# Four-layer transformer on one core: the third attention unrolled, with second k and v buffers, projections spread over all heads and the rotary add moved from Pool to the vector engine

## The reference

```
q = einsum('bim,ghmd->bghid', x, w_aq)     # 4 groups x 4 heads, head size 128
k = einsum('bim,gmd->bgid', x, w_ak)       # one k and v per group
v = einsum('bim,gmd->bgid', x, w_av)
q, k = rope(q), rope(k)                    # even*cos - odd*sin, even*sin + odd*cos
s = einsum('bghid,bgjd->bghij', q*c, k*c)  # causal mask, then softmax over j
r = einsum('bghij,bgjd->bghid', softmax(s), v) @ w_ao
```

## Time and profile before

| | us |
|---|---|
| median of 3 runs | 1525.63 (1524.83 to 1525.65) |
| profiled execution, span from first to last instruction | 1523.4 |
| PE busy | 1347.9 (88%) |
| DVE busy | 740.1 (49%) |
| ACT busy | 618.9 (41%) |
| Pool busy | 113.5 (7%) |

### The profile page before, as it was taken

One profiled execution on the slowest core, in us unless ns is written; L12 is line 12 of the kernel. 1 busy time (PEld: TensorE's weight loads), 2 busy tenths in 40 slices (PEclk: granted clock), 3 DMA queues, 4 the chain that ended last, 5 costly groups with the idle time before them and its releaser, 6 DMA issues.

```text
span 1523.4 us, 21462 instructions
## 1 busy us (share of the span) xinstructions
PE 1347.9 (88%) x6802; PEld 820.4 (54%) x6802; DVE 740.1 (49%) x1677; ACT 618.9 (41%) x1516; POOL 113.5 (7%) x115
## 2 busy tenths in 40 slices
PE   5888888579999996888888889998999999999995
PEld 3633344352345454545455557765666666666863
DVE  4676545431222224776767675024433433434547
ACT  2534433479721111444344342134444444444033
POOL 2410000320000000111111110000000000000000
PEclk9989999759999999999999999999999999999998
DMA  5000000300010001000000000101000000000000
GB/s 138 1 2 1 2 18 0 143 1 0 1 66 0 0 0 73 11 11 7 14 7 14 4 8 0 58 17 61 21 21 10 21 21 10 21 21 1 1 1 28
DMA packets 17558, 31.75 MB, mean 21 GB/s; under 512 B 3049, under 2 KB 15177, under 8 KB 16356
## 3 DMA queue, kind: packets, MB, share of 16 engines
q1 hardware_dynamic: 17076, 28.94, 5.6%
q0 software_dynamic: 432, 2.16, 0.7%
HBM read 32.11 MB, written 1.05 MB: 22 GB/s over the span
## 4 chain that ended last, share of the span: by engine, by line
PE 61%; issue 23%; DVE 8%; ACT 3%; POOL 3%; SPq 0%; DMA 0%; POOLq 0%; DVEq 0%; ACTq 0%
PE bank L719 9%; PE bank L833 8%; PE bank L746 6%; PE bank L729 5%; PE bank L694 5%; PE bank L714 4%; PE bank L853 4%; PE bank L613 3%; PE bank L597 3%; PE bank L738 3%; POOL R L436 2%; PE bank L514 2%; DVE W L1315 1%; PE bank L885 1%; PE bank L568 1%
## 5 line engine op out<-in xcount | busy, mean ns | idle before, releaser
L1393 DVE TENSOR_REDUCE nm<-bank 128x1 f32<-128x128 f32 (+3 forms) x256 | 124.7, 487 | 200.0 <-PE bank L730 199.8
L909 ACT COPY R<-bank 128x512 f32<-128x512 f32 (+4 forms) x184 | 107.6, 609 | 273.9 <-PE bank L694 113.7
L719 PE MATMUL bank<-XNT,W 128*128 128x512 f32 x416 | 203.8, 614 | 16.1 <-POOL R L436 12.4
L1054 ACT ACTIVATE R<-bank,nm 128x128 f32<-128x128 f32 (+3 forms) x256 | 137.9, 539 | 173.7 <-DVE nm L1393 173.5
L729 PE MATMUL bank<-R 128*128 128x128 f32 (+3 forms) x512 | 182.5, 440 | 0.8 <-DVE R L1422 0.8
L746 PE MATMUL bank<-PT,R 128*128 128x512 f32 (+3 forms) x512 | 151.3, 438 | 2.5 <-issue 2.5
L1402 DVE TENSOR_SCALAR R<-R,erec 128x128 f32<-128x128 f32 (+3 forms) x256 | 132.7, 518 | 9.0
L738 PE MATMUL bank<-identf,R 128*128 128x128 f32 x640 | 112.8, 275 | 24.7 <-DVE R L1402 22.6
L746 PEld LDWEIGHTS bank<-PT,R 128*128 128x128 f32 x512 | 93.9, 191 | 74.9 <-issue 54.6
L1017 ACT ACTIVATE PT<-bank 128x512 f32<-128x512 f32 (+3 forms) x256 | 109.7, 519 | 47.4 <-PE bank L602 41.4
L909 ACT COPY PT<-bank 128x128 f32<-128x128 f32 (+3 forms) x256 | 110.7, 434 | 40.7 <-PE bank L738 40.3
(11 more groups left out here) (196 smaller groups left out, 1698.5 us busy)
## 6 DMA issues: line engine op xcount, KB each, us to landing
W<-in_wq SPq DMA_DIRECT2D x32, 128.0 KB, 2.0
W<-in_wo SPq DMA_DIRECT2D x2, 2048.0 KB, 8.1
W<-in_wk SPq DMA_DIRECT2D x20, 128.0 KB, 2.1
W<-in_wv SPq DMA_DIRECT2D x20, 128.0 KB, 2.0
W<-in_wa SPq DMA_DIRECT2D x2, 1024.0 KB, 5.4
W<-in_wb SPq DMA_DIRECT2D x2, 1024.0 KB, 7.2
W<-in_ed SPq DMA_DIRECT2D x1, 1792.0 KB, 14.6
W<-in_eg SPq DMA_DIRECT2D x1, 1760.0 KB, 7.0
```

Source lines behind the costliest of these rows:

```text
L719: ins = mm(bank[:, :], wqkv23[:, 0 if kind == "q" else 1, c, :], XNT[:, c, b * SEQ:(b + 1) * SEQ], start=c == 0, stop=c == DC - 1)
L909: return nc.scalar.copy(dst, src)
L1054: fn(Pr[u % 4][:, 0:n], PS[u % 4][:, 0:n], ACT.Exp, bias=nm[:, u % 4:u % 4 + 1], accum_out=esum[:, u % 4:u % 4 + 1]).then_inc(ca["e_ready" ...
L1393: dve.tensor_reduce(nm[:, u % 4:u % 4 + 1], PS[u % 4][:, 0:(u % TPB + 1) * P], AX.X, ALU.max, negate=True).then_inc(ca["nm"], 1)
```

## The change

- `attention23(l)` becomes two functions, `attention2` and `attention3`. The third attention is written out, 128 steps without a loop, with waits on constants. The fourth keeps its loop, its table and its order.
- The six first projections come in the order q, k of batch 0, q, k of batch 1, v, v, into banks 6, 7, 4, 5, 6, 7, and all of them before the first scores.
- Later projections all go into bank 7. Every head but the last has the q of the next head at v = 0 (batch 0) and v = 4 (batch 1); in each head of the first three groups one of the next group's k, k, v, v stands at v = 2.
- k and v have a second buffer (`ks2`, `vv2`, by group), and the rotation two pairs of temporaries (`rope_t`, `rope_u`).
- A rotation is wholly on DVE: three products, a wait for their end, then the add. A bank is free for the next projection after the products (`rope_mul`); the scores wait for the add (`qk_ready`). Pool has no part in the loop. The normalisation stays on DVE with the same two operations.
- SP has a semaphore for each of q, k and v weights and loads each after its last reader.

```
-        KV2_STEPS = {0: ("q", 0), 2: ("k", 0), 3: ("q", 1), 5: ("k", 1), 6: ("v", 0), 7: ("v", 1)}
-        Q_STEPS = {2: ("q", 0), 6: ("q", 1)}
+        PJ2 = [("q", 0, 0, 6), ("k", 0, 0, 7), ("q", 1, 0, 4), ("k", 1, 0, 5), ("v", 0, 0, 6), ("v", 1, 0, 7)]
+        N_FIRST = len(PJ2)
+        EVENT2 = {}
+        for head in range(NH):
+            g, h = head // GROUP, head % GROUP
+            for v in (0, 2, 4):
+                if v != 2 and head + 1 < NH:
+                    EVENT2[head * TILES + v] = len(PJ2)
+                    PJ2.append(("q", v // 4, head + 1, 7))
+                if v == 2 and g + 1 < KV2:
+                    EVENT2[head * TILES + v] = len(PJ2)
+                    PJ2.append(("kv"[h // 2], h % 2, g + 1, 7))
...
+            for e, (kind, b, i, bank) in enumerate(PJ2):      # SP
+                if b == 0:
+                    continue
+                if kind == "q" and i + 1 < NH:
+                    sp.wait_ge(pj_ps, e + 1)
+                    sp.dma_start(wqkv23[:, 0], wq[i + 1]).then_inc(wq_in, 16)
...
-            def rope_add(n, dst):                              # Pool
-                pool.wait_ge(ca["rope_a"], n + 1)
-                pool.tensor_tensor(dst, ropet, ropeu, ALU.add).then_inc(ca["pj_used"], 1)
...
+            def attention2():                                  # PE
+                def free(e):
+                    kind = PJ2[e][0]
+                    if kind == "v":
+                        pe.wait_ge(v_ready, nth_v(e) + 1)
+                    else:
+                        pe.wait_ge(rope_mul, nth_qk(e) + 1)
+                def project(e):
+                    kind, b, i, bank = PJ2[e]
+                    same = [x for x in range(e) if PJ2[x][3] == bank]
+                    if same:
+                        free(same[-1])
...
+                def turn(u):
+                    pe.wait_ge(ca["p_ready"], u + 1)
+                    if u >= 2:
+                        pe.wait_ge(ca["pt_sb"], u - 1)
...
+                for e in range(N_FIRST):
+                    project(e)
+                for u in range(4):
+                    scores(u)
+                for u in range(STEPS2):
+                    turn(u)
+                    if u + 4 < STEPS2:
+                        scores(u + 4)
+                    if u in EVENT2:
+                        project(EVENT2[u])
+                    if u % TPB == TPB - 1:
+                        values(u)
...
+                for u in range(STEPS2):                        # ACT
+                    if u + 3 < STEPS2:
+                        exponent(u + 3)
+                    if u % TPB == 0 and u > 0:
+                        store_output(u // TPB - 1)
+                    if u - 1 in EVENT2:
+                        store_v(EVENT2[u - 1])
+                    store_pt(u)
...
+                def rotate2(e):                                # DVE
+                    kind, b, i, bank = PJ2[e]
+                    if kind == "v":
+                        return
+                    n, x, hf = nth_qk(e), PS[bank], DH // 2
+                    t, u = rope_t[n % 2], rope_u[n % 2]
+                    dve.wait_ge(ca["pj_ps"], e + 1)
+                    tt(t, x[:, :], rope2[:, 0, :], ALU.mult)
+                    tt(u[0:hf, :], x[hf:, :], rope2[hf:, 1, :], ALU.mult)
+                    tt(u[hf:, :], x[0:hf, :], rope2[0:hf, 1, :], ALU.mult).then_inc(rope_mul, 1)
+                    dve.wait_ge(rope_mul, n + 1)
+                    tt(qs[b] if kind == "q" else ks2[i % 2][b], t, u, ALU.add).then_inc(qk_ready, 1)
+                for e in range(N_FIRST):
+                    rotate2(e)
+                for u in range(4):
+                    maximum(u)
+                inverse(0)
+                inverse(1)
+                for u in range(STEPS2):
+                    if u + 2 < STEPS2:
+                        inverse(u + 2)
+                    if u + 4 < STEPS2:
+                        maximum(u + 4)
+                    if u in EVENT2:
+                        rotate2(EVENT2[u])
```

More of the change, by code:

```diff
@@ L294, in _ @@
                 sp.dma_start(t, W[s]).then_inc(ld["ffn1"], 16)
[L295 to L327, removed]
@@ L697, in out_projection, with v_tiles @@
                 pe.wait_ge(s_ready, NT * l + 6)
[L699 to L703, removed]
+            def v_tiles(bank, b):
+                for t in range(TPB):
+                    for c in range(DC):
+                        ins = mm(bank[:, t * P:(t + 1) * P],
+                                 XNT[:, c, b * SEQ + t * P:b * SEQ + (t + 1) * P], wqkv23[:, 2, c, :],
+                                 start=c == 0, stop=c == DC - 1)
+                return ins
@@ new lines, in qk_tile, with score_tile @@
+            def qk_tile(bank, s, b):
+                for c in range(DC):
+                    ins = mm(bank[:, :], wqkv23[:, s, c, :], XNT[:, c, b * SEQ:(b + 1) * SEQ],
+                             start=c == 0, stop=c == DC - 1)
+                return ins
+            def score_tile(u, q, k):
+                t = u % TPB
+                n = (t + 1) * P
+                mm(PS[u % 4][:, 0:n], q[:, t * P:n], k[:, 0:n], start=True, stop=False)
+                return mm(PS[u % 4][:, t * P:n], identb[:, :], mask_qk[:, :], start=False, stop=True)
@@ L710, in project @@
                         pe.wait_ge(ca["pj_used"], n + 1 - ahead)
[L711 to L720, removed]
+                    ins = v_tiles(bank, b) if kind == "v" else qk_tile(bank, 0 if kind == "q" else 1, b)
@@ L1424, in body @@
                 def body(i, last):
                     k = 0
-                    for h in range(hb):
-                        for v in range(TILES):
-                            u = h * TILES + v
-                            if u + 2 < nt or not last:
-                                normalise(i * nt, u + 2)
-                            if u + 4 < nt or not last:
-                                maximum(i * nt, u + 4)
-                            ev = plan[h].get(v)
-                            if ev and not (last and h == hb - 1):
-                                store_projection(ev[0], ev[1], i * npj + 6 + k, PS[7])
-                                k += 1
@@ L1438, in attention23 @@
-                k = 0
+                    for v in range(TILES):
+                        if v + 2 < nt or not last:
+                            normalise(i * nt, v + 2)
+                        if v + 4 < nt or not last:
+                            maximum(i * nt, v + 4)
+                        if v in PLAN3 and not last:
+                            if PLAN3[v][0] == "k":
+                                store_k(PLAN3[v][1], i * npj + 6 + k, PS[7])
+                            k += 1
                 for b in range(B):
-                    for kind in "qkv":
-                        store_projection(kind, b, k, PS[6 + k % 2], (qs if kind == "q" else ks)[b])
-                        k += 1
+                    store_k(b, 3 * b + 1, PS[7 - b])
@@ L1447, in attention23 @@
                 normalise(0, 1)
[L1448 removed]
+                with dve.Fori(0, NH - 1) as i:
                     body(i, False)
[L1450 removed]
+                body(NH - 1, True)
             def ffn01(l):
```

339 lines of the change are left out of this document (208 added, 131 removed).

## The result

The changed kernel takes 1546.84 us (median of 4 runs, 1538.93 to 1547.45), the kernel before 1525.64 beside it (1524.83 to 1527.06): a ratio of 1.0113, 95% interval 1.0085 to 1.0142. It is slower, by 21.2 us at the medians. The profiled executions differ by as much, 1544.7 against 1523.4 us.

The account below looks back on a forecast made before the run. TensorE was taken to bound the third attention. Half heads +28.0, start -2.7 and end -1.1 gave +24.2 us; with 4 for the clock, 1525.6 + 24.2 + 4 = 1554 us, range 1541 to 1572.

Parts of the forecast that it names:

- What bounds the stage, and what the old order hides: Third attention: TensorE bounds it; with q at t = 2, 3.7 us of TensorE work and the next t = 0 cover the rotation.
- The ceiling of 44 us: Third attention: TensorE idles 43.7 us, so a change altering no matmul can win some 44 us there at most.
- The last comer at the old wait: Old half head, turn of t = 2: the 1.12 us wait, named after the normalisation, ended with ScalarE's copy of tile 0.
- Removed: Third attention: 36 Pool adds of 1.26 us go, with slowed normalisations (about 32 us of vector engine) and 12.4 us of waits.
- The half head, laid out to 10.87: Each new half head of the third attention: 10.87 us, with 3.17 us idle in place of 1.12; stage difference +28.0.
- A k projection is free, a v projection delays the turn by 0.45: Projections at t = 2: k fits before the values; each of six v projections delays tile 3's turn by about 0.45 us.
- The two cancel: Rival: in the third attention's 30 halves values do not wait for ScalarE, -33.6 us, total 1524; chance 0.05.
- One finish decides: Third attention: vector engine finishing tile 3 before 3.98 in the layout would mean a gain; plain order gives 5.97.
- Start and end: Stage edges: four rotations in a row at the start, -2.7 us; the last head's first half loses a stall, -1.1.
- The clock, 4 us in the stage: Third attention: new stalls may drop TensorE's clock to 1.2 GHz; bounds nothing to 32 us lost, 4 us taken.
- The move from Pool pays: Rival: order costs nothing in the third attention, idle time goes; 1480 us, or 1503 with half the waits; chance 0.06.
- The clock falls in most halves: Rival: stalls returning with every half of the third attention lower the clock, +24 + 32, total 1582 us; chance 0.12.

Follow-up runs that it names:

- e4: The changed kernel with q projections back at v = 2 and 6, k or v at v = 4, and ScalarE copying before it exponentiates: 1480.89 us, ratio 0.967.
- e1: The changed kernel with only the q projections moved back to v = 2 and 6, k or v at v = 4: 1502.83 us, ratio 0.9791.
- e10: The kernel before with ScalarE's copy ahead of the exponential in the third attention only: 1511.31 us, ratio 0.9893.
- e6: The kernel before with the loop of the third attention written out on every engine, nothing else: 1531.33 us, ratio 1.0014.
- e7: The kernel before, third attention written out, rotary add moved from Pool to the vector engine, old placement and single k and v buffers: 1519.75 us, ratio 0.9923.
- e2: The changed kernel with only ScalarE's order turned round, copy of a turned tile ahead of the next exponential: 1517.2 us, ratio 0.9908.
- e5: The changed kernel with each rotation one step later on the vector engine, behind the next normalisation, projections staying at t = 0: 1532.92 us, ratio 1.0006.
- e3: The changed kernel with the loop's adds back on Pool, placement of the change kept: 1567.06 us, ratio 1.0206.
- e8: The changed kernel with q projections at v = 2 and 6, k or v at v = 4, and the loop's adds on Pool: 1509.31 us, ratio 0.9851.
- a_again: The changed kernel, unaltered, run once more with a profile: span 1544.1 us, 318.07 us for the 30 halves.
- e9: The changed kernel with the loop's adds on Pool and the scores of every t = 2 tile computed twice: 1555.23 us, ratio 1.0162.

## Why the prediction was right, and where it was off

The forecast, 1554 us, is 7.2 above the measured 1546.84; the direction and the mechanism were right, and the sizes were off. That the total lies so near, and in the range at all, is partly luck. For the edited stage 24.2 us were forecast and 12.8 measured, the 4 us for the clock did not come in the halves, and 8.5 us came in unedited code, where zero was counted. Without these 8.5 the time would have been 1525.6 + 12.8 = 1538.4, below the stated 1541.

**What bounds the stage, and what the old order hides: right.** With TensorE's work unchanged (1141 matmuls against 1140 in the 30 halves) the time moved mostly with its idle time. The ceiling of 44 us was too low: e4 took 46.3 from the halves alone, where only 40.8 were idle, because the same matmuls are busy for 250.79 us there and for 260.06 before. Why their busy time differs was not tested. That q at t = 2 hides the rotation and q at t = 0 does not is shown by e1 alone: 45.4 us for the placement.

**The last comer at the old wait: right, against the name in the profile.** The earlier trace rows names the normalisation; the copy of tile 0 ended at 713.66 and the turn began at 713.80. e10 moved only ScalarE's exponential, and the wait went.

**Removed: right in kind, and not priced.** The 256-column normalisation went from 1.26 to 0.354 us, and Pool's row is gone. The prediction never priced that gain by itself. Parts in a chain, by the 30 halves: 300.91 (e6), 284.30 with the adds on the vector engine (e7), 271.35 with second buffers and spread projections as well (e1), 316.80 with q at t = 0 (after). That is -16.6, -13.0 and +45.4. What the buffers and the spreading give singly was not taken apart.

**The half head, laid out to 10.87: the mechanism right, the term too large by 0.41.** Against the layout, from the half's start in the timeline above: first product 2.36 (2.41), the add's slot 0.61 (0.75), turn of tile 3 at 5.84 (6.03) behind an idle time of 1.76 (2.05), maximum of 384 columns 6.42 (6.70), exponential 7.00 (7.30), copy 7.58 (7.88), values 8.20 (8.61) behind 0.80 (1.12), end 10.46. Most of it are small gaps between instructions that were rounded upward: the add was given 0.75 with its wait, and the reciprocal starts 0.61 after it (738.10 - 737.49), before its 0.69 are over, and TensorE started 0.05 after the copy and not 0.14. 30 x 0.41 = 12.3 us, which is the whole miss of the sum: 28.0 - 12.3 = 15.7 against 15.96. This is the mis-sized term. "A k projection is free, a v projection delays the turn by 0.45": the median of all halves holds the k halves, and a half with v takes 10.95, 0.49 more. Two counts in the prediction are off, without weight in its sum: there are six k and six v projections in the 30 halves, so 18 halves have neither, not 19, and the rival "The two cancel" had 12 k projections to show where there are six, 2 us and not 4.

**One finish decides: half the story.** The prediction bound everything to the vector engine's finish of tile 3. e2 leaves that finish where it was and still takes 25.2 us away, and e5 takes that wait away and gets 40.4 us before the values, where the kernel after has 21.1. Two finishes decide, the normalisation for the turn and the copy for the values. Both were in the layout, but not in the sentence drawn from it.

**Start and end.** -1.76 for -2.7, and -1.37 for -1.1. The start ran at a grant of 0.88; in e1, e2, e3, e4 and e5 the same start took 15.15 us, and in the kernel after once more 15.14 at a grant of 1.00, which is -3.55 (e8 had 16.94 too, again at 0.88). The gain was undersized, and the clock took half of it back here. "First turn near 610" failed (616.91), mostly because the stage itself began 5.9 us later. "TensorE's idle time in the stage near 70 us" was 60.6 (329.59 - 268.99).

**The clock, 4 us in the stage: wrong place.** In the 30 halves the grant was 1.00 (0.99 in a_again), so stalls of 1.76 and 0.80 us per half cost no clock there. Outside the stage, where zero was counted, 8.5 us came. One instance is in the fourth attention of the kernel after, by stretch and on the timeline:

```profile
1057.00:1063.00 6.00, 5.88 (x10) 2.60 (x11) 0.00 (x0) 0.67 (x2) 0.00 (x0) 0.63 0.00 0
```

```profile
1057.12 5.84 PE L729 MATMUL bank<-XNT,W 128*128 128x512 f32 x8 [0.67 <-ACT XNT L988]
```

In the kernel before they take 3.70 us:

```profile
1038.08 3.70 PE L719 MATMUL bank<-XNT,W 128*128 128x512 f32 x8 [0.68 <-ACT XNT L909]
```

The instructions are the same; at a grant of 0.63 they run mostly at the lower level. Whether these 8.5 us belong to the change stays open. For it: the 5.9 us ahead of the stage came twice, and there the three profiles with the loop in place took 594.07 to 596.02 us, and all eleven of longer programs 596.34 to 603.84. Against it: e6, a longer program with the old order, is at 1.0014 [0.9997, 1.003], so 5 us at most and perhaps nothing; and the kernel before alone went from 1524.35 to 1537.81 us over its runs.

**The rivals.** "The move from Pool pays" failed for the kernel as changed. Its mechanism is real in size, and e1 (1502.83) and e4 (1480.89) landed where its two times (1503 and 1480) were put, once the projection was placed so that the rotation is covered. In part that is chance: by their ratios to the kernel before, and from 1525.6, they stand at 1494 and 1475, and e4 has ScalarE's order changed too. The rule that sends two-input adds to VectorE (Trainium skill, GPSIMD Engine Reference, 4.1 Engine selection) is borne out by e7 against e6 (16.6 us) and by e1 against e8 (6.8 us). The place of the projections, which decides what stands behind the add, was worth 45.4 us here. "The two cancel": its condition, values that do not wait for ScalarE, was made true by e2, which took 1517.2, 7 us under the 1524 given (by its ratio 1512, 12 under). "The clock falls in most halves" did not come; e3, with 0.3 us more of stall in a half, shows how near it was: there it came in 12 of the 30 halves, most of all where no k or v projection stands between the stalls.

## What to carry to other kernels

Before moving work to a less loaded engine, write out what then stands behind it on that engine's queue and how much the bounding engine can do meanwhile: the same instructions gave 0.979 or 1.011 of the old time by their place alone. Put the producer where independent matmuls follow that are longer than its whole chain. A wait for several semaphores is named after one of them in the profile; compare end times of all candidates with the start (here a copy ended 0.14 us ahead), and look at which instruction waits, since in e1 one name stood for another wait than in the kernel after. Where two things arrive nearly together repair both, since e1 and e2 alone left 18 and 37 us of idle time and together 3.7.

## What the runs showed of the hardware

A vector-engine product beside Pool's add is slowed by more than the add costs on the vector engine itself: 256 columns 0.35 to 1.26 us, 512 columns 0.49 to 1.39, each 0.9 more, and the add 0.69.

TensorE's clock can turn a small stall into a large one. With stalls of 1.76 and 0.80 us in a half head of 10.46 the grant stayed at 1.00, with some 2.1 and 0.8 in 10.76 it was 0.93, and 0.75 in halves of the last group, and additional matmuls brought it back and the time down by 17.7 us (e3 and e9). Where exactly the border lies was not measured.

The same program's unedited first part took 2 us more in another execution (594.09 and 596.02, in the kernel after 599.97 and 602.02), and the whole kernel before spread over 13 us between runs on three chips. A difference of 8 us in unedited code is therefore not to be explained from two traces.
